# Three instead of four down-projection weight buffers, and three instead of four key blocks in a banded attention, in a fused attention and expert-FFN kernel

## What is computed

```python
xn = layernorm(x)
# attention with fixed gaussian weights, 8 heads of 128 columns
v = xn @ input_weights.T
probs[h,q,k] = gauss(k - q - offset[h], std[h])    # std 1,2,4,8; offset -1,-2,-4,-8
s = einsum('hqk,bhkd->bhqd', probs, v) @ output_weight.T
# 8 experts, 1024 -> 4096 -> 1024, all summed
acc = 0
for wg, wu, wd in experts:
    acc += (silu(xn @ wg) * (xn @ wu)) @ wd
out = x + s * silu(acc)
```

## Time and profile before

| | us |
|---|---|
| timed runs (2) | 6256.92 and 7187.28, median 6722.1 |
| the profiled execution | 6269.43 |
| its span on the slowest core, core 7 | 6268.4 |
| the spans of the other cores | 6223.1 to 6260.0 |
| from the start of pass 0 to that of its last down phase | 114 to 1944 |
| its last down phase and passes 1 to 3 | 1944 to 6016 |
| the attention's and the last stages | 6016 to 6268 |

### The profile page before, as it was taken

One profiled execution on the slowest core, in us unless ns is written; L12 is line 12 of the kernel. 1 busy time (PEld: TensorE's weight loads), 2 busy tenths in 40 slices (PEclk: granted clock), 3 DMA queues, 4 the chain that ended last, 5 costly groups with the idle time before them and its releaser, 6 DMA issues.

```text
span 6268.4 us, 66674 instructions; the slowest of 8 cores (6223.1 to 6268.4 us)
## 1 busy us (share of the span) xinstructions
PE 5622.2 (90%) x26056; PEld 2539.6 (41%) x26056; DVE 1019.6 (16%) x1493; ACT 668.7 (11%) x1159; POOL 594.5 (9%) x796
## 2 busy tenths in 40 slices
PE   3767777777778999999999999999999999999986
PEld 2323333333333444444444444444444444444444
DVE  4010111111111111111111111111111111111124
ACT  0000000000000111111111111111111111111120
POOL 1111111111111000000000000000000000000000
PEclk9988989988989999999999999999999999999998
DMA  7999999999998565555556656665666555555533
GB/s 151 172 184 160 189 185 167 181 185 166 180 178 183 148 155 151 150 152 150 152 153 150 152 148 155 148 155 148 155 148 154 151 150 152 150 152 154 138 58 115
DMA packets 562911, 974.84 MB, mean 156 GB/s; under 512 B 29744, under 2 KB 291888, under 8 KB 562608
## 3 DMA queue, kind: packets, MB, share of 16 engines
q0 software_dynamic: 407808, 406.90, 46.7%
q1 hardware_dynamic: 154800, 563.68, 25.0%
HBM read 1234.70 MB, written 142.61 MB: 220 GB/s over the span
## 4 chain that ended last, share of the span: by engine, by line
PE 76%; DMA 20%; DVE 1%; issue 1%; POOL 1%; SPq 0%; ACT 0%; DVEq 0%; POOLq 0%; ACTq 0%
PE psum L357 27%; PE psum L331 23%; PE psum L339 23%; DMA wub<-wu 13%; DMA wdb<-wd 3%; DMA wus<-wub 3%; DMA x_t<-x 1%; PE psum L437 1%; PE psum L463 0%; POOL wgb L233 0%; DVE H_sb L376 0%; DVE x_t L515 0%; PE psum L180 0%; DVE xn_b L165 0%; DMA wio_sb<-wo 0%
## 5 line engine op out<-in xcount | busy, mean ns | idle before, releaser
L331 PE MATMUL psum<-xnT,wgb 128*128 128x512 bf16 x8192 | 1994.7, 388 | 290.4 <-DMA wub<-wu 286.8
L357 PE MATMUL psum<-wdb,H_sb 128*128 128x512 bf16 x8192 | 1788.6, 381 | 190.8 <-DMA wdb<-wd 150.9
L339 PE MATMUL psum<-xnT,wub 128*128 128x512 bf16 x8192 | 1958.3, 382 | 0.0
L331 PEld LDWEIGHTS psum<-xnT,wgb 128*128 128x128 bf16 x8192 | 806.7, 99 | 1310.8 <-issue 390.6
L357 PEld LDWEIGHTS psum<-wdb,H_sb 128*128 128x128 bf16 x8192 | 803.7, 98 | 1175.7 <-issue 228.9
L376 DVE TENSOR_TENSOR H_sb<-xc,psum 128x512 bf16<-128x512 f32 x1024 | 703.8, 687 | 3135.1 <-PE psum L339 3131.1
L339 PEld LDWEIGHTS psum<-xnT,wub 128*128 128x128 bf16 x8192 | 809.6, 99 | 994.7 <-issue 50.1
L369 ACT ACTIVATE xc<-psum 128x512 f32<-128x512 f32 x1024 | 611.5, 597 | 5227.5 <-PE psum L331 5227.5
L248 POOL DMA_DIRECT2D wdb<-wd x512 | 360.1, 705 | 4309.3 <-PE psum L357 4284.2
L386 DVE TENSOR_TENSOR g_sb<-g_sb,psum 128x512 f32<-128x512 f32 x224 | 136.4, 680 | 1666.6 <-PE psum L357 1666.6
L233 POOL DMA_DIRECT2D wgb<-wg x128 | 113.0, 883 | 1103.0 <-PE psum L339 559.7
(11 more groups left out here) (36 smaller groups left out, 276.9 us busy)
## 6 DMA issues: line engine op xcount, KB each, us to landing
wdb<-wd POOLq DMA_DIRECT2D x512, 512.0 KB, 6.9
wgb<-wgs SPq DMA_DIRECT2D x384, 512.0 KB, 4.7
wub<-wus SPq DMA_DIRECT2D x384, 512.0 KB, 5.6
wgb<-wg POOLq DMA_DIRECT2D x128, 512.0 KB, 18.1
wub<-wu POOLq DMA_DIRECT2D x128, 512.0 KB, 30.6
wgs<-wgb SPq DMA_DIRECT2D x128, 512.0 KB, 8.6
wus<-wub SPq DMA_DIRECT2D x128, 512.0 KB, 11.4
x_t<-x SPq DMA_DIRECT2D x35, 512.0 KB, 4.1
```

The source lines that it names most:

```text
L331: inst = nc.tensor.matmul(ba, wg_buf(gidx % 4)[:, jc, 128 * ci:128 * (ci + 1)], xnT[:, jc, tok0:tok0 + T_PASS], start=(jc == 0), stop=(jc ...
L339: inst = nc.tensor.matmul(bu, wu_buf(gidx % 4)[:, jc, 128 * ci:128 * (ci + 1)], xnT[:, jc, tok0:tok0 + T_PASS], start=(jc == 0), stop=(jc ...
L357: inst = nc.tensor.matmul(bank(grp), H_sb[:, c, 128 * t:128 * (t + 1)], wd_buf(par)[:, c % G, 512 * dh:512 * (dh + 1)], start=(c == 0), st ...
```

## The change

The down weights have three buffers instead of four: two in `wdb`, one in `wdb2`, chosen by `gidx % 3`, with three landing semaphores; a load now waits for the consumption of the group three before it. `wdb2` is half as large (4 KB instead of 8 KB of each partition), and the buffers allocated behind it lie 4 KB lower. In the attention the first of the four key blocks is left out (the keys 129 to 255 and more before the query, whose weights are vanishingly small for a standard deviation of at most 8 and an offset of at most 8); `ptab` is still built for four.

```diff
-        s_dwld = [Sem(es, nc, f"s_dwld{i}") for i in range(4)]
+        s_dwld = [Sem(es, nc, f"s_dwld{i}") for i in range(3)]
...
-        wdb2 = es_ffn.enter_context(nc.sbuf_tensor("wdb2", [128, 2, G, D], BF16))
+        wdb2 = es_ffn.enter_context(nc.sbuf_tensor("wdb2", [128, 1, G, D], BF16))
...
-            return wdb[:, par, :, :] if par < 2 else wdb2[:, par - 2, :, :]
+            return wdb[:, par, :, :] if par < 2 else wdb2[:, 0, :, :]
...
-                dpar = gidx % 4
-                if dpar >= 2 and first_d2:
+                if par == 2 and first_d2:
                     nc.gpsimd.wait_ge(s_xnT.h, NT)
                     first_d2 = False
-                if gidx >= 4:
-                    ep, k = divmod(gidx - 4, NGRP)
+                if gidx >= 3:
+                    ep, k = divmod(gidx - 3, NGRP)
...
-                s_dwld[dpar].inc(nc.gpsimd.dma_start(wd_buf(dpar), src), 16)
+                s_dwld[par].inc(nc.gpsimd.dma_start(wd_buf(par), src), 16)
...
-                    par = gidx % 4
+                    par = gidx % 3
                     if c % 2 == 0:
-                        nc.tensor.wait_ge(s_dwld[gidx % 4].h, 16 * (gidx // 4 + 1))
+                        nc.tensor.wait_ge(s_dwld[gidx % 3].h, 16 * (gidx // 3 + 1))
...
-                    for di in range(NDELTA):
+                    for di in range(1, NDELTA):
...
-                            start=(di == 0), stop=(di == NDELTA - 1))
+                            start=(di == 1), stop=(di == NDELTA - 1))
```

## The result

The changed kernel takes 6323.3 us (median of 11 runs, the lowest 6310.25); the ratio to before is 1.0096, with a 95% interval from 1.0075 to 1.0117. That is about 60 us slower, under the 2% bound, and less than half of what was forecast (6408, +139). The chip runs one die or both at a lower clock in some executions; the ratios here, and the cores read in experiment 9, leave those out. The profiled execution took 6310.28 us, its slowest core is core 0 with 6309.2.

A forecast was written before the change was run, and what follows sets the result against it. DMA was taken to set the pace in pass 0, TensorE in passes 1 to 3. Passes 1 to 3 +101, pass 0 +37, its expert 7 +8, attention -7: +139 on 6269.4 gives 6408 us, range 6315 to 6500.

The forecast's parts named there:

- first rival: Down phases: landings shrink to 5.0 us once waits thin the stream, so none waits; +22, 6291 us; chance 0.14.
- second rival: Pass 0: up loads bound each expert, so it takes up its share of the cost; +94, 6363 us; chance 0.12.
- The limit of 6.09 us: Passes 1 to 3, three buffers: a wdb load is in time if it lands within 6.92 - 0.70 - 0.13 us.
- I take the median of these very loads: Passes 1 to 3: median landing 6.9 us is 0.81 late, five waits a phase, 24 phases at 4.2 us, 101 us.
- The scatter: Down phases of passes 1 to 3: landings of 5.0 to 8.4 us add, thinner stream takes away; +0.1 us for both.
- the forecast's signs of being wrong: Landings under 6.1 us, waits not at every third group, clock drop in passes 1 to 3, or pass 0 ending unchanged.
- Pass 0, 5.3 us an expert: Experts 0 to 6: 3.46 us later issue plus 1.8 us of waits, 7 x 5.3 = 37 us.
- I see no slack that takes it up: Pass 0: the 5.3 us an expert stays in full, since the queue then holds one wdb load only.
- Expert 7 of pass 0: SP's reloads slow its first down loads; group 6 starts 5 us later, three more waits of 0.8; 8 us.
- the attention: Query-block pitch falls from 2.24 to 1.82 us, VectorE then deciding; 16 blocks, 7 us gained.
- The clock: Passes 1 to 3: TensorE's new waits, mostly under 1.5 us, leave the clock at 1.00.
- fourth rival: Passes 1 to 3: waits bring TensorE's clock down, 288 us more, 6696 us; chance 0.04.

The follow-up runs named there:

- experiment 9: The changed kernel run once more, unaltered, beside experiment 8 on the same chip; its one comparable timed run is 6358.91 us, no ratio formed.
- Experiment 3: Kernel before, four buffers and old attention, but each down load waits for the group three before it instead of four; ratio to before 1.0115.
- experiment 1: Changed kernel with the attention's four key blocks restored, so three down-weight buffers alone; lowest time 6323.74 us, no ratio formed.
- experiment 2: Kernel before with only the attention's first key block left out, four down-weight buffers kept; ratio to before 0.9997.
- experiment 6: Against experiment 1: the next expert's up groups 0 and 1 are listed after down group 12 instead of 13; ratio to before 1.0112.
- experiment 5: Against experiment 2: all 16 down loads of an expert listed before the next expert's up groups 0 and 1; ratio to before 1.0008.
- experiment 7: Against experiment 1: the three down-weight buffers' memory cut into six half-size buffers, each loaded and released by itself; ratio to before 1.0027.
- experiment 8: Experiment 7's six half-size down-weight buffers together with the shortened attention of experiment 2; ratio to before 1.0012.
- Experiment 4: Against experiment 1: two down-weight buffers instead of three, attention as before; lowest time 7060.16 us.

## Why the prediction was wrong, point by point

- **Direction and mechanism.** Slower, by waits of TensorE for wdb in passes 1 to 3, at clock 1.00, and a longer pass 0: right. Experiment 3 shows that the later issue alone makes all of the FFN's part. The size, +139 against about +60, is wrong by more than half: 6323 lies inside the range (6315 to 6500) but at its lower end, between the first rival's 6291 and the second's 6363, and within the 2% that I gave 0.37.
- **The limit of 6.09 us** (6.92 less 0.70 and 0.13): right. The first load of a down phase starts 0.70 us after the release in the changed kernel as well, and with two buffers the same method gives 19.4 us of waiting an expert where 19.9 were measured, though in 11 waits and not 7.
- **The failed step: "I take the median of these very loads", 6.9 us.** It was mis-sized twice. It was core 7's, and the eight cores' mean was 6.4 in that same trace; by the forecast's own arithmetic 5 x 0.31 x 24 = 37 us would have come out instead of 101 (that this is near the measured 36 is luck, by what follows). And it was measured with four buffers, where nothing ever waits and the queue is at its fullest; with three it is 6.05. The measured cost is 1.51 us a phase (mean of 192 phases), 3.5 stops of 0.43 us, where the forecast had 5 of 0.81.
- **The scatter** was set at 0.1 us a phase, taken together with the thinner stream. With the median of 6.05 just under the limit a formula by the median gives nothing, so all of the 1.51 is scatter: it should have been a term of its own. Two of the forecast's signs of being wrong came true by this: landings under 6.1 us, and waits at other groups than every third.
- **The first rival** (the landings shrink once waits thin out the stream) was given 0.14 and was half right. Its end value, 5.0 us, isn't reached, since waits of 1.5 us a phase thin the stream little; but the loop seems to close on itself: a late load makes a wait, the wait empties the queue, the next loads land sooner. With two buffers it went down to 5.4.
- **Pass 0, 5.3 us an expert:** measured 2.5 (17.6 / 7). Beside each other on one chip, experiments 1 and 3 are 17 and 19 us a pass longer than 2, experiment 6 is 11 longer than 5 and 7, and 9 only 4 longer than 8, with cores 30 us and more apart in each. The failed step is "I see no slack that takes it up". In the down phase nearly all of the 5.3 came, 4.5 us, and the up phase gave 2.0 back. The wait for group 14 stood on the chain, but the second rival had it right that the DMA engines, with a share of 1.05, set the pace of an expert; experiment 5 took that whole wait away and won nothing. Why 2.5 us remain is argued only: a wait in the down phase for want of a buffer is time in which a full queue would have moved bytes. Experiment 4, with 18.6 us of such waits and 22.9 us an expert, agrees; it wasn't tried by itself.
- **Expert 7 of pass 0:** 4.2 us instead of 8: on core 7 group 3 waits 4.66 us as foretold, but the waits of the groups behind it didn't come; **the attention:** 8.3 instead of 7. The pitch is 1.78 instead of 1.82, because the next cast starts 0.04 us before the copy's end; 16 x 0.46 is 7.4, and the other 0.9 is open.
- **The clock:** right on average; it dropped once each on two cores, behind waits of 2.2 and 2.9 us, and experiment 4, with waits of 2 to 5.8 us, shows the fourth rival's mechanism. **No change for SBUF places and semaphores:** right, by experiment 3.

## What to carry to other kernels

When a buffer is taken from a ring, compare two numbers: the time from a buffer's release to the need for its next load, and the landing time, read on every core and not on the slowest. Here they lay within a microsecond of each other, and the landing time that counted was the one with the smaller ring, which was shorter; the cost was then the scatter, not the difference of the medians. Cutting the same memory into finer pieces bought the margin back. And a DMA wait on the chain of a stage whose DMA engines are full need not be time that can be won: here removing the longest one won nothing, while new waits for want of a buffer still cost.

## What the runs showed of the hardware

- The landing time of the same 512 KB load changed with the number of buffers: medians of 6.4, 6.05 and 5.4 us with four, three and two, at 194 to 198 ns a packet in each case. Within the kernel before it was 6.9 us with two earlier loads under way and 6.2 with one.
- With four buffers the median differs between cores of one execution, from 5.7 to 7.0 us, and the core with 6.9 was core 7 in one execution and core 2 in another. With waits in the loop this spread is small (6.0 to 6.3). What sets a core's place in that spread is open.
- Splitting the loads in two left passes 1 to 3 as long as with four full buffers (3845.4 and 3846.5 us against 3845.1): 32 issues a phase instead of 16, medians of 5.1 to 5.5 us for half the bytes in experiment 7. Over the whole kernel its ratio is 1.0027 (1.0002 to 1.0052).
